# Five rotating PSUM banks in the retention, and feed-forward weights cast to bf16 ahead of time on the odd cores

## The chip, the cores and the metric

The kernel runs on the 8 cores of one Trainium2 chip as one program. The metric is the device time in microseconds of the slowest core. The runs of the kernel before took 2073.68, 2083.73 and 2284.54 us, median 2083.73.

## The reference

The input is `x`, four sequences of 2048 tokens by 2048 channels. What is computed:

```
xn = layernorm(x)
s  = retention(xn)          # 16 heads of 128: q, k, v = xn @ w_qkv; rotary tables on q and k;
                            # scores q k^T with a decay mask, causal; y = scores v;
                            # per-head norm (mean, variance); silu(xn @ w_g) * y; @ w_proj
r  = argmax(xn @ w_router)  # per token: one of three paths
g  = silu( path 0: xn + bias
           path 1: xn + (xn @ w_down^T) @ w_up^T
           path 2: transformer layer: layernorm, softmax attention (16 heads), residual,
                   layernorm, gelu(x @ w_ff1^T) @ w_ff2^T (8192 hidden), residual )
out = x + s * g
```

The weights come as float32 in DRAM. Products run in bf16. Path 2 is computed only for the tokens that take it (its queries and its feed-forward); its keys and values need every token of the sequence.

## The kernel before, in words

**Split.** Each sequence belongs to two cores. The even core (`FIRST`, names `a_`) has the first 1280 tokens, with 10 token tiles of keys and 10 of its own rows; the odd core (`SECOND`, names `b_`) has the last 768 tokens as its own and all 16 tiles of keys. The path-2 tokens are packed into 464 columns on an even core, 288 on an odd one. A branch on the input `half` picks the share; both are one program text.

**Stages.** (1) Phase 0: layernorm of the token tiles, transposes into `xn`, values of heads 0 to 3, and keys and queries of head 0. (2) Retention, `ret_step(h)` for 16 heads (L886 on). The main products of a step, 16 matmuls each into one PSUM bank (`group`, L252; the matmul is L262), are queries `Q` and keys `K` of head h+1 and the gate `G` of head h-1: 9 on an even core, 8 on an odd. After heads 3, 7 and 11 a burst `ret_vburst` computes the values of the next four heads (10 or 16 more products). (3) Projection `proj`, (4) attention of path 2, `ffn_step`, (5) `wo`, (6) `ff1` and `ff2`: 64 + 64 weight tiles, each of which feeds 16 matmuls of 464 or 288 columns.

**Order inside a step.** `gap(main)` runs one main product, then the deferred small pieces of the one before (`pend`, above all `swap`: the rotary partner product through L269, whose result VectorE multiplies into `swt` and adds), then `late`. Behind each gap come the small events of `ret_events`, at fixed slots: `T` transposes keys (L762), `U` the state (L776), `S(p)` a score pair (L796, L797), `A(p)` scores by values into bank Y (L816 to L822), `M` and `V` mean and variance of the head norm. Every engine executes its own instructions in this order.

**PSUM.** 8 banks: A, B and M rotate (`bank`, L244) among all main products and most small ones; Y takes the attention output; `S[0]` and `S[1]` are pairs of banks, used in turn by the scores (`s = p % 2`) and, `S[1]`, by the key transposes. A product waits until the engine that reads its bank has emptied it (`self.free[k]`). The cosine product `t_c` in `ret_qk` is issued to VectorE right after the main product's copy, ahead of the `swap` of the product before.

**Beside it.** In heads 0 to 3 VectorE also does the router: 80 pieces on an even core, 48 on an odd, two per event from gap 2 of head 0 on, the rest in the burst after head 3. In heads 4 to 11 `h_step` computes the path-1 and path-0 rows, in pairs (`h_first`, 2 small matmuls, L712, and 4 VectorE operations into `hz`): a step's first 6 (4) rows at gap 0, the others at gap nq+1, their silu at gaps nq and nq+2, the next loads at nq+2 and nq+4 (nq is 3 or 2).

**DMA.** Weight tiles are 128 by 2048, 1 MB in float32. GpSimd's queue (POOLq, queue q0) casts them on the way into SBUF, 0.5 MB there. Retention weights go through a ring `wr` of 5 (4) slots: a slot is reloaded when its product is done. The value weights are loaded one quarter per head, at the start of the step. From the last heads of path 2's attention on, `Ring` `wb` streams 16 + 128 tiles (`fo`, `f1`, `f2`) through 21 (28) slots. SyncE's queue (q1) moves rotary tables, router rows and intermediate results.

Of the kernel before, what the change touches and what calls it, by code (L numbers as in the profile page):

```python
# [36 lines left out]
class Share:  # L37
# [18 lines left out]
    wr=[6, 10, 14, 18, 22], xn=26, xt=[86, 66, 74], xk=[94, 98], og=66,  # L56
# [13 lines left out]
    wr=[6, 10, 14, 18], xn=22, xt=[86, 94, 102], xk=[110, 114], og=86,  # L70
# [66 lines left out]
class Ring:  # L137
# [17 lines left out]
    def load(self):  # L155
        while self.next < len(self.plan):
            k = self.next
            if k < self.n:
                if k not in self.opened:
                    return  # L160
                toks = self.opened[k]
            else:
                before = self.plan[k - self.n][0]
                if before not in self.freed:
                    return
                toks = (self.freed[before],)
            key, src = self.plan[k]
            t = self.kern.dma("pool", self.stream[k % self.n], self.tile[k % self.n][:, :], src,
                              *toks)
            self.got[key] = (self.tile[k % self.n], t)  # L170
            self.next += 1
# [6 lines left out]
class Kern:  # L178
# [92 lines left out]

    def gap(self, main):


        due, self.pend = self.pend, []
        main()
        for f in due:
            f()
        late, self.late = self.late, []
        for f in late:  # L280
            f()
# [7 lines left out]
    def build(self):  # L289
# [22 lines left out]
        self.xc_sp = dint("xc_sp", [CT, P, W])  # L312
        self.r_sp = dint("r_sp", [16, P], F32)
# [39 lines left out]
        self.S = [nc.alloc_psum_tensor(f"S{i}", [P, 2, W], F32) for i in range(2)]  # L353

# [28 lines left out]
    def run(self, s):  # L383
        nc = self.nc
        self.g, self.tag = s, s.name + "_"
        self.free = {k: None for k in "ABMY"}
# [46 lines left out]
    def phase0(self):  # L433
# [88 lines left out]
        self.t_p0 = [*xfree, *kfree]  # L522
        self.hq_load(0)
# [20 lines left out]
    def ret_buffers(self):  # L544
# [38 lines left out]
        self.main_last = None  # L583

# [13 lines left out]
    def ret_qk(self, kind, h, c, piece, col, w, dst):  # L598
# [13 lines left out]
        t_c = self.op("dve", "tt", dst, qb, tab[:, 0, 0:w], op=ALU.mult,  # L612
                      toks=(t_b, self.t_tab[h, piece], used))
        tmp = self.swt[n % 2][:, 0:w]

# [138 lines left out]
    def ret_kturn(self, h):  # L754

        n = self.g.parts[1][1]
        kk = self.kk[h % 2]
        out = self.S[1].ap().rearrange("p a n -> p (a n)").bitcast(BF16)[:, 0:n * P]
        self.wait("pe", self.Sfree[1], *[self.t_qk["k", h, c]
                                         for c, (col, w) in enumerate(self.g.kc) if col < n * P])  # L760
# [5 lines left out]
        self.t_kt = self.Sfree[1] = self.op("act", "act", self.kt[:, :], out, AF.Copy,  # L766
                                            toks=(tp, self.kt_used))
# [17 lines left out]
    def ret_score(self, h, p):  # L785
        g = self.g
        c, j, skip, w = g.pairs[p]
        s = p % 2
        S, n = self.S[s], self.nsc
# [3 lines left out]
        self.wait("pe", self.Sfree[s], self.t_qk["q", h, c], self.t_qk["k", h, j * P // W],  # L793
# [5 lines left out]
        self.Sfree[s] = self.op("dve", "tt", self.sc[n % 4][:, :, 0:w], S[:, :, 0:w],  # L799
                                self.mk[:, :, 0:w], op=ALU.mult, toks=(ts, self.sc_used[n % 4]))  # L800
        self.t_sc[h, p] = (self.Sfree[s], n % 4)
# [65 lines left out]
    def ret_events(self, h):  # L867
# [7 lines left out]
        if last == 2:  # L875
            ev = [[T], [S(0)], [S(1), U], [S(2), A(0)], [S(3), A(1)], [S(4), A(2)],
                  [A(3), M(0)], [A(4)], [V(0), M(1)], [], [V(1), M(2)], [], [V(2)]]
        else:
            ev = [[S(0)], [T], [S(1)], [U], [S(2)], [A(0)], [A(1)], [A(2)],
                  [M(0)], [], [V(0), M(1)], [], [V(1)]]  # L880
        return ev

    def ret_step(self, h):
# [25 lines left out]
        n = len(mains)  # L909
        steps = nq * 2 + len(g.kc)  # L910
        ev = self.ret_events(h)
        rest = self.ret_events(h - 1)[steps:] if h > 0 else []
        now = [(ev[k] + (rest[k] if k < len(rest) else [])) for k in range(steps)]
        by_gap = [[e for k, e in enumerate(now) if k * n // steps == a] for a in range(n)]
        for a, main in enumerate(mains):
# [8 lines left out]
            for e in by_gap[a]:  # L924
                if h < 4 and (h > 0 or a >= 2):
                    self.router_piece()
                for f in e:
                    f()
                if h < 4 and (h > 0 or a >= 2):
# [248 lines left out]
    def proj(self):  # L1178
# [44 lines left out]
        for k in range(n):  # L1223
# [4 lines left out]
            if rest and k > 0:  # L1228
                rest.pop(0)()
            if k >= 1:  # L1230
# [61 lines left out]
    def ffn_buffers(self):  # L1292
# [27 lines left out]
        if r > 0:  # L1320
            self.ffn_ring(r, self.t_x1c)
        plan = ([(f"fo{k}", self.wd["fo"][k]) for k in range(16)] +
                [(f"f1{k}", self.wd["f1"][k]) for k in range(FT)] +
                [(f"f2{k}", self.wd["f2"][k]) for k in range(FT)])
        self.big = Ring(self, f"wb{r}", "wb", [kb for part in m["big"] for kb in part], plan)
# [362 lines left out]
    def ff1(self):  # L1688
# [13 lines left out]
        self.wait("pe", *self.free.values(), *self.Sfree)  # L1702
# [147 lines left out]
```

How the kernel before makes its waits and increments, by code:

```python
    def wait(self, e, *toks):  # L197
        for tok in toks:
            if tok is None:
                continue
            s, v = tok
            if self.met[e].get(s.name, 0) < v:
                self.eng[e].wait_ge(s, v)
                self.met[e][s.name] = v
# [1 line left out]
    def done(self, e, inst):  # L206
        s = self.sem[e]
        inst.then_inc(s, 1)
        self.count[s.name] += 1
        return (s, self.count[s.name])
# [1 line left out]
    def dma(self, e, stream, out, in_, *toks, **kw):  # L212
        if stream not in self.dsem:
            self.dsem[stream] = self.new_sem("d_" + stream)
        s = self.dsem[stream]
        self.wait(e, *toks)
        self.eng[e].dma_start(out=out, in_=in_, **kw).then_inc(s, 16)
        self.count[s.name] += 16
        return (s, self.count[s.name])
# [1 line left out]
    def indirect(self, stream, out, out_at, in_, in_at, *toks, **kw):  # L221
        if stream not in self.dsem:
            self.dsem[stream] = self.new_sem("d_" + stream)
        s = self.dsem[stream]
        self.wait("pool", *toks)
        self.nc.gpsimd.indirect_dma_start(out, out_at, in_, in_at, **kw).then_inc(s, 16)
        self.count[s.name] += 16
        return (s, self.count[s.name])
```

## Time and profile before

| | us |
|---|---|
| runs | 2073.68, 2083.73, 2284.54 |
| profiled execution, time | 2068.31 |
| its spans, cores 0 to 7 | 1995.6, 2062.9, 1994.6, 2063.2, 1997.9, 2066.7, 1988.3, 2064.5 |
| granted TensorE clock, even / odd cores | 0.966 to 0.970 / 0.955 to 0.957 |
| core 5 (slowest): TensorE busy | 1749.7 |
| core 5: VectorE, ScalarE, GpSimd busy | 825.2, 678.1, 174.1 |

The span of a core is from its first to its last instruction. "Idle before" is the time an engine stood still just ahead of an instruction, and the releaser is what it waited for. A matmul's recorded length overlaps its neighbours, so the pitch from start to start is its cost in a full stream. The DMA share is the mean busy share of the core's 16 DMA engines.

### The profile page before, as it was taken

How to read it: one execution, taken by the hardware profiler on the slowest of the kernel's cores; microseconds unless marked ns; L12 is line 12 of the kernel's file. 1: busy time of each engine (PE TensorE's matmuls, PEld its weight loads, DVE VectorE, ACT ScalarE, POOL GpSimd, SP SyncE). 2: the span in 40 equal slices, each digit the busy share in tenths (PEclk: the TensorE clock that was granted, in tenths of full speed). 3: DMA queues.
4: the chain of work that ended last, by engine and by line, in shares of the span. 5: the costliest groups of instructions: out<-in, count | busy, mean ns of one | idle time of the engine just before them, and what ended most of it. 6: DMA issues, size and time to landing. Idle time of an engine off the chain costs nothing.

```text
span 2066.7 us, 28135 instructions; the slowest of 8 cores (1988.3 to 2066.7 us)
## 1 busy us (share of the span) xinstructions
PE 1749.7 (85%) x10020; PEld 954.1 (46%) x10020; DVE 825.2 (40%) x1502; ACT 678.1 (33%) x1099; POOL 174.1 (8%) x309
## 2 busy tenths in 40 slices
PE   4885689788897789987889999999999788876886
PEld 2442344444444344443344455555554456644554
DVE  4635671344414442242621356665657742000000
ACT  2431341233304431344752344444444523110000
POOL 0000000000000000000000000000001121211211
PEclk9996899999999999999999999999999989999998
DMA  8666751355645541432572435545435499999998
GB/s 205 216 95 159 178 143 31 66 106 104 143 142 106 110 92 34 91 83 51 116 169 51 87 67 94 101 87 108 87 67 108 78 173 171 170 165 170 200 213 164
DMA packets 105643, 247.95 MB, mean 120 GB/s; under 512 B 13970, under 2 KB 41874, under 8 KB 103314
## 3 DMA queue, kind: packets, MB, share of 16 engines
q0 software_dynamic: 42672, 149.18, 42.5%
q1 hardware_dynamic: 60754, 96.79, 16.7%
q8 instruction: 87, 1.43, 0.3%
q14 instruction: 66, 0.54, 0.1%
q10 hardware_dynamic: 2064, 0.01, 0.1%
HBM read 361.92 MB, written 27.67 MB: 189 GB/s over the span
## 4 chain that ended last, share of the span: by engine, by line
PE 69%; DVE 9%; ACT 6%; issue 6%; DMA 5%; another core or an unknown queue 4%; SPq 0%; DVEq 0%; POOL 0%; POOLq 0%; ACTq 0%
PE pA L262 20%; PE pM L262 17%; PE pB L262 16%; ACT L247 2%; PE pB L1751 2%; PE pM L1751 2%; DMA b_tab<-tab 1%; DVE b_t L247 1%; PE pA L1751 1%; ACT b_rs L247 1%; DVE b_lt L247 1%; PE pM L1197 1%; DVE bst L456 1%; DMA b_wrh<-wr 1%
## 5 line engine op out<-in xcount | busy, mean ns | idle before, releaser
L262 PE MATMUL pA<-b_vw,b_xn 128*128 128x512 bf16 x800 | 182.7, 382 | 8.6 <-DMA b_vw<-rv 8.6
L262 PE MATMUL pB<-b_xn,b_wr 128*128 128x512 bf16 (+1 forms) x752 | 156.6, 364 | 16.1 <-DVE b_t L247 9.0
L262 PE MATMUL pA<-b_xn,b_wr 128*128 128x512 bf16 (+1 forms) x672 | 147.5, 375 | 12.1 <-DVE b_t L247 8.3
L262 PE MATMUL pM<-b_vw,b_xn 128*128 128x512 bf16 x656 | 149.1, 380 | 0.0
L262 PE MATMUL pM<-b_xn,b_wr 128*128 128x512 bf16 (+1 forms) x656 | 134.3, 360 | 15.4 <-DVE b_t L247 7.3
L247 DVE TENSOR_TENSOR S<-S,b_cb 128x576 f32<-128x576 f32 x128 | 97.0, 760 | 122.5 <-PE S L1421 122.5
L262 PE MATMUL pB<-b_vw,b_xn 128*128 128x512 bf16 x592 | 133.8, 379 | 0.0
L262 PEld LDWEIGHTS pA<-b_vw,b_xn 128*128 128x128 bf16 x800 | 78.5, 98 | 98.7 <-issue 11.3
L262 PEld LDWEIGHTS pB<-b_xn,b_wr 128*128 128x128 bf16 x752 | 74.1, 101 | 86.3 <-issue 33.2
L247 ACT ACTIVATE b_er<-S 128x576 bf16<-128x576 f32 x128 | 83.2, 650 | 77.7 <-DVE S L247 77.3
L247 ACT ACT_TABLE_LOAD x65 | 83.4, 1283 | 63.4 <-PE pA L262 13.7
L262 PEld LDWEIGHTS pA<-b_xn,b_wr 128*128 128x128 bf16 x672 | 66.2, 100 | 82.1 <-issue 25.0
L262 PEld LDWEIGHTS pM<-b_xn,b_wr 128*128 128x128 bf16 x656 | 64.0, 100 | 75.2 <-issue 26.4
L262 PEld LDWEIGHTS pM<-b_vw,b_xn 128*128 128x128 bf16 x656 | 64.2, 98 | 74.6 <-issue 1.1
L262 PE MATMUL pA<-b_xn,b_wf 128*128 128x512 bf16 x416 | 94.0, 379 | 1.1
L217 POOL DMA_DIRECT2D b_wb<-f x128 | 68.2, 552 | 255.0 <-PE pM L262 40.6
L247 DVE TENSOR_TENSOR b_kk<-b_qkb,b_tab 128x512 bf16<-128x512 bf16 x64 | 27.2, 424 | 154.8 <-ACT b_qkb L247 152.2
L262 PEld LDWEIGHTS pB<-b_vw,b_xn 128*128 128x128 bf16 x592 | 57.5, 98 | 66.6 <-issue 0.3
L262 PE MATMUL pM<-b_xn,b_wf 128*128 128x512 bf16 x368 | 83.2, 379 | 0.0
L247 DVE TENSOR_TENSOR b_acc<-b_acc,b_er 128x576 f32<-128x576 f32 x96 | 72.8, 758 | 10.7 <-DVE b_er L247 0.9
L247 ACT ACTIVATE b_sq<-b_t 128x512 bf16<-128x512 f32 (+1 forms) x32 | 16.8, 525 | 140.3 <-DVE b_t L247 137.8
L262 PEld LDWEIGHTS pA<-b_xn,b_wf 128*128 128x128 bf16 x416 | 40.0, 98 | 47.7 <-issue 3.5
(319 smaller groups left out, 2723.5 us busy)
## 6 DMA issues: line engine op xcount, KB each, us to landing
b_wb<-f POOLq DMA_DIRECT2D x128, 512.0 KB, 68.9
b_tab<-tab SPq DMA_DIRECT2D x96, 256.0 KB, 4.0
b_xt<-xp SPq DMA_DIRECT2D x10, 1024.0 KB, 7.7
b_vw<-rv POOLq DMA_DIRECT2D x16, 512.0 KB, 10.4
b_wr<-rq POOLq DMA_DIRECT2D x16, 512.0 KB, 7.3
b_wr<-rk POOLq DMA_DIRECT2D x16, 512.0 KB, 5.9
b_wr<-rg POOLq DMA_DIRECT2D x16, 512.0 KB, 5.9
xn_sp<-b_xn SPq DMA_DIRECT2D x4, 2048.0 KB, 16.0
```

Source lines behind the costliest of these rows:

```text
L217: self.eng[e].dma_start(out=out, in_=in_, **kw).then_inc(s, 16)
L247: return self.done(e, f(*args, **kw))
L262: inst = self.nc.tensor.matmul(self.pb[k][:, 0:w], lhs(ct), rhs(ct), start=(ct == 0), stop=(ct == CT - 1))
L456: ins = nc.vector.bn_stats(b[:, 6 * q:6 * q + 6], xt[n % 3][:, q * W:(q + 1) * W])
L1197: self.nc.tensor.matmul(self.pb[b][:, :], self.og[:, hh, i * P:(i + 1) * P], w[:, hh, :], start=(hh == 0), stop=False)
L1751: ins = nc.tensor.matmul(self.pb[b][:, 0:sl], w[:, (ft % 16) * P:(ft % 16 + 1) * P], self.hg[ft][:, :], start=(ft == 0), stop=(ft == FT - 1))
```

## The change

- Once phase 0 is over, the two banks of `S[1]` join the rotation as X and Z, until the seventh unit of the projection (`pair_to_banks`, `banks_to_pair`). Scores and key transposes all use `S[0]`.
- The cosine product moves behind the `swap` of the product before (`late`).
- `h_first` comes one pair per gap instead of in bursts; the second silu and the load of the next columns' constants come at gap nq+3.
- Events of the head before come ahead of this head's; `M` and `V` events move one or two slots.
- Router pieces start with gap 6 of head 0. Head 0 has 6 gaps, so they start with head 1. In the value burst after head 3 all copies of values are ScalarE's.
- On odd cores (`cast=96`) the steps of heads 2 to 13 each issue, ahead of their main products, 8 DMAs on GpSimd's queue that cast a float32 tile in DRAM to a bf16 tile in DRAM (`fb_sp`). These 96 tiles are `f1` 16 to 63 and `f2` 0 to 47. The ring `wb` later loads them from there; `fo`, `f1` 0 to 15 and `f2` 48 to 63 stay float32.

```diff
-    wr=[6, 10, 14, 18, 22], xn=26, ...
+    wr=[6, 10, 14, 18, 22], cast=0, xn=26, ...
-    wr=[6, 10, 14, 18], xn=22, ...
+    wr=[6, 10, 14, 18], cast=96, xn=22, ...
...
+    def pair_to_banks(self):
+        self.free["X"] = self.free["Z"] = self.Sfree[1]
+        self.rot += ["X", "Z"]
+
+    def banks_to_pair(self):
+        self.wait("pe", self.free["X"], self.free["Z"])
+        self.rot = [k for k in self.rot if k in "ABM"]
+        self.Sfree[1] = None
...
+        self.fb_sp = dint("fb_sp", [96, P, C])
...
+        self.pb["X"], self.pb["Z"] = self.S[1][:, 0, :], self.S[1][:, 1, :]
...
+    def cast(self):
+        n = len(self.t_cast)
+        if 8 * n >= self.g.m["cast"]:
+            return
+        for k in range(8 * n, 8 * n + 8):
+            t = self.dma("pool", f"cast{n % 3}", self.fb_sp[k], self.ff_tile(k),
+                         self.t_cast[n - 3] if n >= 3 else None)
+        self.t_cast.append(t)
+
+    def ff_tile(self, k):
+        n = 16 + k
+        return self.wd["f1"][n] if n < FT else self.wd["f2"][n - FT]
+
+    def ff_plan(self):
+        plan = [(f"fo{k}", self.wd["fo"][k]) for k in range(16)]
+        for n in range(2 * FT):
+            key, src = ...
+            k = n - 16
+            plan.append((key, self.fb_sp[k], self.t_cast[k // 8])
+                        if 0 <= k < self.g.m["cast"] else (key, src))
+        return plan
...
@@ ret_qk
-        t_c = self.op("dve", "tt", dst, qb, tab[:, 0, 0:w], op=ALU.mult,
-                      toks=(t_b, self.t_tab[h, piece], used))
+        t_c = None
+        def cos():
+            nonlocal t_c
+            t_c = self.op("dve", "tt", dst, qb, tab[:, 0, 0:w], op=ALU.mult,
+                          toks=(t_b, self.t_tab[h, piece], used))
+        self.late.append(cos)
@@ h_step
-        if gap in (0, nq + 1):
-            for u in list(then if gap else first)[::2]:
-                self.h_first(u)
-        if gap in (nq, nq + 2):
+        for u in [u for k, u in enumerate(first[::2]) if k == gap]:
+            self.h_first(u)
+        for u in [u for k, u in enumerate(then[::2]) if k == gap - nq - 1]:
+            self.h_first(u)
+        if gap in (nq, nq + 3):
...
-        if gap == nq + 2 and q < 7:
+        if gap == nq + 3 and q < 7:
             self.hq_load(q + 1)
@@ ret_kturn: S[1], Sfree[1] become S[0], Sfree[0]
@@ ret_score
-        s = p % 2
-        S, n = self.S[s], self.nsc
+        S, n = self.S[0], self.nsc
@@ ret_events (first: even cores, second: odd cores)
-                  [A(3), M(0)], [A(4)], [V(0), M(1)], [], [V(1), M(2)], [], [V(2)]]
+                  [A(3), M(0)], [A(4)], [V(0)], [], [M(1)], [], [V(1)], [M(2)], [], [V(2)]]
-                  [M(0)], [], [V(0), M(1)], [], [V(1)]]
+                  [M(0)], [], [V(0)], [M(1)], [], [V(1)]]
@@ ret_step
+        if h >= 2:
+            self.cast()
...
-        now = [(ev[k] + (rest[k] if k < len(rest) else [])) for k in range(steps)]
+        now = [((rest[k] if k < len(rest) else []) + ev[k]) for k in range(steps)]
...
-                if h < 4 and (h > 0 or a >= 2):
+                if h < 4 and (h > 0 or a >= 6):
                     self.router_piece()
@@ ret_vburst
-            self.gap(lambda: self.ret_v(gr, i, "act" if i % 2 else "dve"))
+            self.gap(lambda: self.ret_v(gr, i, "act" if i % 2 or gr == 1 else "dve"))
@@ proj
+            if k == 6:
+                self.banks_to_pair()
```

## Rows read from the trace of the kernel before

**Rows 1.** Spans and granted clocks of cores; core 4 is even, core 5 odd.
```profile
core 4: 1997.9 us, clock 0.966
core 5: 2066.7 us, clock 0.956
```
**Rows 2.** Busy time by stretch, core 5: stretch, length, then each engine, clock, DMA share, GB/s.
```profile
1735.00:1790.00 55.00, 54.96 (x436) 43.38 (x437) 0.00 (x0) 12.24 (x32) 16.32 (x31) 0.97 1.04 172
1790.00:1880.00 90.00, 63.07 (x468) 44.38 (x466) 0.25 (x2) 12.24 (x30) 15.85 (x30) 0.98 1.04 168
1880.00:2051.00 171.00, 138.76 (x1063) 99.49 (x1060) 11.99 (x26) 7.51 (x15) 32.63 (x45) 0.99 1.06 200
```
**Rows 3.** Timeline of core 5's TensorE: start, length, instruction, idle before and its releaser.
```profile
1785.70 2.12 PE L262 MATMUL pA<-b_x2n,b_wb 128*128 128x288 bf16 x16
1787.66 2.12 PE L262 MATMUL pB<-b_x2n,b_wb 128*128 128x288 bf16 x16
...
2048.59 2.12 PE L1751 MATMUL pB<-b_hg,b_wb 128*128 128x288 bf16 x16 [0.33 <-DMA b_wb<-f]
```
**Rows 4.** Busy time by stretch, core 4, final stage.
```profile
1700.00:1800.00 100.00, 100.00 (x515) 50.09 (x514) 2.04 (x5) 15.84 (x27) 16.90 (x32) 1.00 1.04 170
```
**Rows 5.** DMA queues of core 5, whole span: packets, MB, share of 16 engines.
```profile
q0 software_dynamic: 42672, 149.18, 42.5%
q1 hardware_dynamic: 60754, 96.79, 16.7%
```
**Rows 6.** What TensorE of core 4 waited for, 170 to 960 us: total, times, longest.
```profile
PE pM L262 <- ACT a_sil L247: 13.2, 10, 1.6
PE pM L262 <- DVE a_swt L247: 11.9, 12, 2.7
```
**Rows 7.** Busy time of one head step, core 4: with shadow products, then without.
```profile
590.50:634.20 43.70, 36.63 (x206) 19.14 (x205) 25.81 (x52) 21.11 (x37) 2.64 (x5) 0.96 0.52 118
751.40:788.50 37.10, 33.45 (x197) 17.92 (x196) 16.31 (x30) 17.37 (x27) 1.59 (x3) 1.00 0.62 125
```
**Rows 8.** The same two kinds of step on core 5.
```profile
664.50:708.90 44.40, 34.60 (x189) 17.73 (x188) 19.26 (x40) 17.18 (x28) 2.64 (x5) 0.92 0.51 105
880.60:916.80 36.20, 32.14 (x182) 16.70 (x181) 14.06 (x28) 15.35 (x22) 1.58 (x3) 0.95 0.40 88
```
**Rows 9.** Timeline of core 4 about a score: VectorE's queue and TensorE's bank wait.
```profile
614.61 1.91 PE L262 MATMUL pM<-a_xn,a_wr 128*128 128x256 bf16 x16 [1.60 <-ACT a_sil L247]
615.24 0.48 DVE L247 SCALAR_TENSOR_TENSOR a_hz<-pA,msk,a_hk 128x256 f32<-128x256 f32 x1
...
616.46 0.27 PE L797 MATMUL S<-a_qq,a_kk 128*128 128x256 bf16 x1
...
620.16 0.69 DVE L247 TENSOR_TENSOR a_sc<-S,cblk 128x512 bf16<-128x512 f32 x1
```
**Rows 10.** What VectorE waited for, core 5, 141 to 400 us.
```profile
DVE b_qq L247 <- DMA b_tab<-tab: 29.6, 1, 29.6
...
DVE b_rj L247 <- DMA b_wrh<-wr: 10.7, 3, 6.1
```
**Rows 11.** One router piece on VectorE, core 5.
```profile
183.87 1.28 DVE L247 SCALAR_TENSOR_TENSOR b_rj<-b_rx,mv,b_wrh 128x1024 bf16<-128x1024 f32 x1
```
**Rows 12.** DMA queues of core 5, 664.5 to 708.9 us.
```profile
q0 software_dynamic: 719, 2.16, 30.2%
q1 hardware_dynamic: 2721, 2.46, 20.3%
```
**Rows 13.** GpSimd's issues of one head step, core 5.
```profile
699.48 0.53 POOL L217 DMA_DIRECT2D b_vw<-rv  x1 [0.26 <-issue]
709.15 0.53 POOL L217 DMA_DIRECT2D b_wr<-rg  x1 [9.13 <-PE pB L269]
719.29 0.53 POOL L217 DMA_DIRECT2D b_wr<-rk  x1 [9.61 <-PE pA L262]
```
**Rows 14.** Main products of a value burst in the chain of waits, core 5.
```profile
830.71 3.45 PE pM L262 x16
```

More of the change, by code:

```diff
@@ L55 @@
               [(0, 512), (512, 512), (1024, 256)], [(0, 4), (4, 8)], [0, 1, 2], dict(
-    wr=[6, 10, 14, 18, 22], xn=26, xt=[86, 66, 74], xk=[94, 98], og=66,
+    wr=[6, 10, 14, 18, 22], cast=0, xn=26, xt=[86, 66, 74], xk=[94, 98], og=66,
     rx=78, wrh=86, rj=98, xkh=100, iota=84, sel=86, hz=96, nhz=6, hk=102,
@@ L69 @@
                [(1280, 512), (1792, 256)], [(0, 10), (10, 14)], [1, 2], dict(
-    wr=[6, 10, 14, 18], xn=22, xt=[86, 94, 102], xk=[110, 114], og=86,
+    wr=[6, 10, 14, 18], cast=96, xn=22, xt=[86, 94, 102], xk=[110, 114], og=86,
     rx=92, wrh=100, rj=112, xkh=114, iota=98, sel=100, hz=106, nhz=4, hk=110,
@@ L166, in load @@
                 toks = (self.freed[before],)
-            key, src = self.plan[k]
+            key, src, *ready = self.plan[k]
             t = self.kern.dma("pool", self.stream[k % self.n], self.tile[k % self.n][:, :], src,
-                              *toks)
+                              *toks, *ready)
             self.got[key] = (self.tile[k % self.n], t)
@@ L385, in run @@
         self.g, self.tag = s, s.name + "_"
-        self.free = {k: None for k in "ABMY"}
+        self.free = {k: None for k in "ABMYXZ"}
         self.Sfree = [None, None]
@@ L522, in phase0 @@
         self.t_p0 = [*xfree, *kfree]
+        self.pair_to_banks()
         self.hq_load(0)
@@ L583, in ret_buffers @@
         self.main_last = None
+        self.t_cast = []
+    def cast(self):
[12 more added lines that the diff above has]
+        for n in range(2 * FT):
+            key, src = (f"f1{n}", self.wd["f1"][n]) if n < FT else (f"f2{n - FT}",
+                                                                   self.wd["f2"][n - FT])
+            k = n - 16
+            plan.append((key, self.fb_sp[k], self.t_cast[k // 8])
+                        if 0 <= k < self.g.m["cast"] else (key, src))
+        return plan
     def vw_load(self, which, g, tok, pieces=range(4)):
@@ L757, in ret_kturn @@
         kk = self.kk[h % 2]
-        out = self.S[1].ap().rearrange("p a n -> p (a n)").bitcast(BF16)[:, 0:n * P]
-        self.wait("pe", self.Sfree[1], *[self.t_qk["k", h, c]
+        out = self.S[0].ap().rearrange("p a n -> p (a n)").bitcast(BF16)[:, 0:n * P]
+        self.wait("pe", self.Sfree[0], *[self.t_qk["k", h, c]
                                          for c, (col, w) in enumerate(self.g.kc) if col < n * P])
@@ L765, in ret_kturn @@
         self.kk_used[h % 2] = tp
-        self.t_kt = self.Sfree[1] = self.op("act", "act", self.kt[:, :], out, AF.Copy,
+        self.t_kt = self.Sfree[0] = self.op("act", "act", self.kt[:, :], out, AF.Copy,
                                             toks=(tp, self.kt_used))
@@ L792, in ret_score @@
         q = self.qq[h % 2][:, col:col + w]
-        self.wait("pe", self.Sfree[s], self.t_qk["q", h, c], self.t_qk["k", h, j * P // W],
+        self.wait("pe", self.Sfree[0], self.t_qk["q", h, c], self.t_qk["k", h, j * P // W],
                   self.t_qk["k", h, (j + 1) * P // W])
@@ L798, in ret_score @@
             S[:, 1, 0:w], kk[:, (j + 1) * P:(j + 2) * P], q, start=True, stop=True))
-        self.Sfree[s] = self.op("dve", "tt", self.sc[n % 4][:, :, 0:w], S[:, :, 0:w],
+        self.Sfree[0] = self.op("dve", "tt", self.sc[n % 4][:, :, 0:w], S[:, :, 0:w],
                                 self.mk[:, :, 0:w], op=ALU.mult, toks=(ts, self.sc_used[n % 4]))
-        self.t_sc[h, p] = (self.Sfree[s], n % 4)
+        self.t_sc[h, p] = (self.Sfree[0], n % 4)
         self.qq_used[h % 2] = self.kk_used[h % 2] = ts
@@ L928, in ret_step @@
                     f()
-                if h < 4 and (h > 0 or a >= 2):
+                if h < 4 and (h > 0 or a >= 6):
                     self.router_piece()
@@ L1321, in ffn_buffers @@
             self.ffn_ring(r, self.t_x1c)
[L1322 to L1325, printed above, removed]
+        self.big = Ring(self, f"wb{r}", "wb", [kb for part in m["big"] for kb in part],
+                        self.ff_plan())
     def big_open(self, part, *toks):
@@ L1701, in ff1 @@
                 [self.S[s][:, a, 0:sl] for s in (1, 0) for a in range(2)])
-        self.wait("pe", *self.free.values(), *self.Sfree)
+        self.wait("pe", *[self.free[k] for k in "ABMY"], *self.Sfree)
         for ct in range(CT):
```

## The prediction

> **What bounds the kernel now.** First the spans: the odd cores end last, 2066.7 us against 1997.9 on the even core of the same pair [rows 1]. So 68.8 us of any gain on odd cores count, and beyond that both kinds must gain.
>
> Next the busy time by stretch of the odd core's feed-forward. TensorE is busy 54.96 of 55 us up to 1790, then 63.07 of 90 and 138.76 of 171, while the DMA share stays at 1.03 to 1.06 [rows 2]. The timeline says how long a weight tile takes TensorE when nothing is missing: starts at 1785.70 and 1787.66, a pitch of 1.96 us. At the end each tile waits for its load [rows 3]. From 1790 on the odd core waits for weights. The even core, with 464 columns per tile, is busy 100.00 of 100 us there [rows 4]: nothing in this stage can speed it up.
>
> Then the retention. A head step of the even core takes 43.70 us with 36.63 busy; without the small products of path 0 and 1 it takes 37.10 with 33.45 busy [rows 7]. On the odd core it is 44.40 with 34.60 at a clock of 0.92, and 36.20 with 32.14 [rows 8]. The waits of the even core name readers of banks A, B and M: ScalarE's silu and VectorE's rotary product [rows 6]. TensorE is ready and lacks a bank.
>
> **The tail of the odd core.** Queue q0 moved 149.18 MB, as written, in 42.5% of 2066.7 us, so a tile of 0.524 MB costs 3.09 us [rows 5]. That is what a cast load costs. An uncast bf16 tile is not in this queue; half as many bytes are read for it, so 1.54 us is one bound. The other is queue q1's rate, which includes its small packets: 345 us for 96.79 MB, 1.87 us per tile [rows 5]. Both are below 1.96, so the choice changes nothing: TensorE sets the pace. From 1735 us 120 tiles remain, which end at 2051 now [rows 2]. At 1.96 us they take 235, and 48 transposes about 5: 1735 + 240 = 1975, **76 us less**. The last 16 float32 tiles need 49 us of DMA against 31 of products, but 28 slots let them start 28 x 1.96 = 55 us early. Their cover is gone only if the ring starts late.
>
> **Five banks and the new order.** For the even core the floor of a step is its busy time at full clock, 36.63 x 0.96 = 35.2 us [rows 7]. Against it stands the single score pair. Today a score ends at 616.73 and its mask product at 620.85, 4.1 us later, since VectorE has `hz` operations of 0.48 us ahead of it [rows 9]. With two pairs nobody waits for that. With one, the next score or key transpose does. In the new order the VectorE work of gap 0 or 1 adds up to about 5.4 us (rotary 1.5, one pair of rows 2.0, mean 0.7, mask 1.2), and the next product is partly the 256-column one, so about 2 us per step stay lost. I take 37.0 for the even core: 8 steps x 6.7 = 54 us. In heads 12 to 14 `h_first` is absent; I take 34.7, which gives 3 x 2.4 = 7. Head 0 sheds 12 router pieces of 1.28 us [rows 11], which return in the value burst, where ScalarE takes over the copies; I take 8. The 29.6 us wait for a rotary table [rows 10] stays, since that load stands behind the same router loads. Sum **70 us**: 1998 to 1928. The bounds are 85 (no pinch) and 20 (a pinch in most gaps).
>
> On the odd core the same working gives 34.60 x 0.92 = 31.8, with the pinch and some hiccups 34.5: 8 x 9.9 = 79; heads 12 to 14 to 32, 3 x 4 = 12; head 0 8. Sum 99, before the casts.
>
> **The casts.** GpSimd issues 8 x 0.53 us per head; it stood idle 9 us before its next issue, so this hides [rows 13]. The wait on an earlier cast is met a head before. The DMA time does not hide as well. The trace has no DRAM-to-DRAM cast. The nearest row is the cast load, with the same read and the same bytes written: 3.09 us. If the write came on top at q1's rate it would be 3.09 + 1.87 = 4.96. I take 3.1, since in the load too reading and writing run together; nothing excludes less, to the 1.54 of half the work.
>
> In a step the two queues use 30.2 + 20.3% of 44.4 us, 22.4 us [rows 12]. With 24.8 of casts it is 47.2, more than the 34.5 that TensorE would need. Over four heads with a burst of 14 products of 3.45 us, 48 us [rows 14], the demand is 189 us against 186. So the burst pays back, but the three steps before it cannot all be short: 34.5, then about 42 and 45. That returns 18 us per group, 36 in heads 4 to 11. In head 2 of the odd core the second set of router weights now loads amid a cast; VectorE's wait of 10.7 us [rows 10] becomes about 20: 9 us. Sum 45. The odd core keeps 99 - 45 = **54 us** of the retention.
>
> All casts and the next weights share GpSimd's queue. The gate tile of the next step is issued 9.7 us after the step's first load, the key tile 10.1 later [rows 13]. Behind a cast batch they land about 30 us into the step and are needed near 40. The Trainium skill ("DMA: Bandwidth & Descriptors", section SWDGE vs HWDGE vs iDMA) says that only one SWDGE queue is allocated, so this order cannot be escaped; the trace agrees, with all of GpSimd's loads in q0.
>
> **Sum.** Odd: 2066.7 - 76 - 54 = 1937. Even: 1928. The profiled execution took 2068.31, 1.6 more than its span; two of the runs shown lie 5 and 15 above it, the third far off. So 1937 + 1.6 + 10 = 1949, say **1950**.
>
> **Rivals.**
> *Casts are dear (0.14).* The DMA share during the cast heads goes to 1 and TensorE waits for ring tiles. At 4.4 us a cast, a step needs 22.4 + 35.2 = 57.6 us of DMA and a group of four 230, against 226 now (4 x 44.4 + 48): heads 4 to 11 gain nothing. Head 0 and heads 12 to 14 keep 20, head 2 loses 10 and heads 12 and 13, with less DMA of their own, 8. Odd: 2066.7 - 76 - 20 + 18 = 1989, time 2000; at the upper bound 4.96 a group costs 248, 44 more in two groups, time about 2045. For it: the three steps are already short of DMA at 3.1. Against: a tile of the load costs 3.09 us for 1 MB read and half of that written, and q1 1.87 for as much written and half as much read [rows 5]; that looks like a price set by the longer side. The same page (section Specifications) limits a core to about 358 GB/s of HBM. By it, the 1.57 MB that a cast reads and writes would take 4.4 us, an estimate; the feed-forward's rows, about 170 GB/s written and twice that read, do not contradict it.
> *The score pair takes the place of the banks (0.10).* If VectorE's lag stays at 4.1 us, a score behind a short product waits about 2.4 us, and the order of events forces five such places a step: the even core gains nothing and ends at 1998, time 2010. For it: the pair is used by five scores and a transpose. Against: the bursts of `h_first`, which cause the lag, are gone.
> *Slower: the casts cost far more than a load (0.06).* Place: queue q0 in heads 2 to 13, 670 us now, of which 12 x 22.4 = 269 are demanded by today's DMAs. The tail's 76 us are eaten at (670 + 76 - 269) / 96 = 5.0 us a cast; 2% slower is 5.4. At 6.2, twice the load, it is 864 us: time about 2190. Against it: the row bound is 4.96.
> *The tail is not relieved (0.04).* If the ring still arrives late, for instance because bf16 tiles cost near 3 us, only the retention gains: 2067 - 54, time about 2025.
>
> **Chances.** My forecast has 0.66. What a measurement here can tell from no change is about 2%, 42 us: faster means below 2042. Of the rivals the dear casts fall mostly there (0.09 of 0.14), the pair and the tail almost wholly: faster 0.88, same 0.06, slower 0.06. Range: low, no loss to the casts and no pinch, where the even core at 1913 decides: 1905 allows for its last microseconds. High, the pair rival and the middle of the dear casts: 2025.
>
> **What would show it.** Right: on odd cores the feed-forward from 1735's counterpart on at a pitch of 1.96 us per tile, DMA share well under 1 there; head steps of 37 us on the even core, 6.7 less than now; on the odd core short steps after a burst and longer ones before the next, with waits on `wr` tiles; both kinds of core within 30 us of each other. Wrong: TensorE waiting for `wb` loads still, L796 or L762 waiting for VectorE's `sc` more than 3 us a step, cast DMAs that take over 4 us each in the queue, or rotary tables that land so late beside them that the odd core's steps are over 44 us.

## The result, and the profile after

The changed kernel takes 2172.08 us (median of 4 runs, 2143.39 to 2332.38) where the kernel before takes 2088.01 in the same session (4 runs): the ratio is 1.0316, with an interval of 1.0228 to 1.0404. It is slower; 1950 was forecast. The far ends of these ranges are executions at a lower clock on one die, which the ratios and the mean spans given below leave out and the medians do not.

Spans and granted clocks, to be set against [rows 1]:

```profile
core 6: 2042.5 us, clock 0.949
core 7: 2141.8 us, clock 0.919
```

Core 7 is odd, core 6 even; the other cores of each kind lie within 9 and 6 us of them. The odd core is 75.1 us longer than core 5 before, the even one 44.6 longer than core 4. Both lost, the odd one more.

Where? I cut each core's time at two marks of the timeline: the transposes of the keys of head 0 and of head 15. These are the marks of core 7, then those of core 5 before:

```profile
142.39 0.94 PE L807 MATMUL S<-cblk,b_kk 128*128 128x128 bf16 x14 [2.28 <-DVE b_sc L247]
1104.24 0.94 PE L807 MATMUL S<-cblk,b_kk 128*128 128x128 bf16 x14 [2.56 <-DVE b_sc L247]
```
```profile
141.00 0.94 PE L762 MATMUL S<-cblk,b_kk 128*128 128x128 bf16 x14
950.10 0.94 PE L762 MATMUL S<-cblk,b_kk 128*128 128x128 bf16 x14 [0.83 <-DVE b_kk L247]
```

Before head 0 nothing changed (+1.4 us). Heads 0 to 15 grew from 809 to 962, **+153**. What follows, to the end of the span, shrank from 1116.6 to 1037.6, **-79**. The even core does the heads in 800 us against 767, +33, and what follows in 1146 against 1135, +11.

**The tail.** Busy time by stretch, core 7, answering [rows 2]:

```profile
1900.00:2000.00 100.00, 100.00 (x819) 79.88 (x817) 0.00 (x0) 20.96 (x51) 26.92 (x51) 1.00 0.97 318
2000.00:2100.00 100.00, 100.00 (x836) 80.25 (x835) 10.95 (x25) 7.01 (x14) 28.84 (x43) 1.00 0.87 213
```

From the first tile of `ff1` to the last of `ff2` core 5 takes 237.4 us (1886.3 to 2123.7), against 315.4 before (1735.0 to 2050.4): 78 us less. TensorE is busy 100.00 of 100 us, where core 5 had 138.76 of 171. Its timeline has the pitch of 1.96 us of [rows 3], now without a wait:

```profile
1951.06 2.12 PE L262 MATMUL pM<-b_x2n,b_wb 128*128 128x288 bf16 x16
1953.02 2.12 PE L262 MATMUL pA<-b_x2n,b_wb 128*128 128x288 bf16 x16
```

**The heads of the odd core.** Two steps of core 7, answering [rows 8]; the transposes at their edges are 89.7 and 37.8 us apart:

```profile
421.00:511.00 90.00, 36.20 (x190) 18.80 (x191) 19.64 (x41) 17.05 (x28) 6.55 (x13) 0.71 0.95 150
511.00:548.00 37.00, 33.59 (x205) 18.41 (x202) 20.30 (x45) 16.96 (x28) 6.65 (x13) 0.93 0.51 102
```

The second is the forecast step, 37 us with 33.59 busy. The first has almost the same work and takes 90. The granted clock averages 0.71 over it: TensorE stands still for tens of us and comes back at the lower of its two levels, half of full speed. From 520 us on it is at full speed again:

```profile
507.00:512.00 5.00, 1.26 (x13) 1.29 (x14) 4.62 (x10) 0.90 (x2) 0.00 (x0) 0.50 0.49 159
...
520.00:530.00 10.00, 8.06 (x51) 4.22 (x50) 4.52 (x9) 6.43 (x12) 1.06 (x2) 1.00 0.51 101
```

Step by step against core 7 of experiment 1, the same order without casts: head 2 takes 53 us more, head 4 53, head 6 59, head 10 30, and each of the others 12 or less. Three steps of twelve make two thirds of the loss. Why head 5, with the same eight casts, loses only 3 us is not explained.

What TensorE and VectorE of core 7 wait for, from 170 and from 90 us to 1105:

```profile
PE S L807 <- DVE b_sc L247: 176.7, 15, 48.3
PE S L840 <- DVE b_sc L247: 39.3, 7, 19.3
PE S L756 <- DMA b_hu<-up: 22.8, 2, 13.8
```
```profile
DVE b_hz L247 <- DMA b_hk<-xk_sp: 169.4, 8, 61.0
DVE b_xkh L247 <- DMA xk_sp<-b_xkh: 37.0, 3, 21.6
```

The heaviest lines of the two engines are for the most part one wait. TensorE waits at the transposes (L807) for the mask product that frees the only score pair. That product stands in VectorE's queue behind an `hz` operation, which waits for a tile `hk` of 64 KB, up to 61 us. The timeline of GpSimd, SyncE, VectorE and TensorE in the long step shows the chain:

```profile
456.55 3.89 POOL L217 DMA_DIRECT2D fb_sp<-f  x8 [0.19 <-issue]
...
467.47 38.47 SPq L217 DMA_DIRECT2D b_hk<-xk_sp  x6
...
506.74 0.48 DVE L247 SCALAR_TENSOR_TENSOR b_hz<-S,msk,b_hk 128x256 f32<-128x256 f32 x1 [46.04 <-DMA b_hk<-xk_sp]
...
509.38 1.22 DVE L247 TENSOR_TENSOR b_sc<-S,cblk 128x1024 bf16<-128x1024 f32 x1
...
510.74 1.55 PE L807 MATMUL S<-cblk,b_kk 128*128 128x128 bf16 x13 [37.65 <-DVE b_sc L247]
```

Eight casts are issued at 456. SyncE needs 38 us for six loads of `hk`, since each waits for the store that empties its buffer (`h_sp<-b_hk`), and that store is late as well. What SyncE waited for from 467 to 507 us:

```profile
SPq L203 <- DMA h_sp<-b_hk: 35.5, 6, 18.5
```

VectorE stands 46 us and TensorE 38. The DMA issues of 455 to 512 us (count, KB each, median us to landing) say what was in the way:

```profile
fb_sp<-f POOLq DMA_DIRECT2D x8, 512.0 KB, 30.5
b_tab<-tab SPq DMA_DIRECT2D x4, 256.0 KB, 3.6
...
b_wr<-rg POOLq DMA_DIRECT2D x1, 512.0 KB, 32.1
b_hk<-xk_sp SPq DMA_DIRECT2D x6, 64.0 KB, 31.7
```

**The heads of the even core.** The step that answers [rows 7], and TensorE's waits of 170 to 960 us, which answer [rows 6]:

```profile
568.00:612.00 44.00, 36.37 (x202) 20.03 (x204) 25.38 (x50) 20.32 (x37) 2.64 (x5) 0.92 0.72 76
```
```profile
PE S L840 <- DVE a_sc L247: 102.6, 30, 9.3
...
PE pB L269 <- ACT a_yb L247: 6.4, 3, 5.5
```

The long list of waits for a reader of A, B or M is gone, as planned. One wait for the single score pair has taken its place.

### The profile page after: what moved, and what is told of

Read it like the earlier page. It is cut to its first block, busy times and chain, and to the rows that moved or that the text cites. A ratio compares the mean times of both kernels' runs of the same rounds, so it can differ in the third digit from the quotient of the medians.

```text
span 2141.8 us, 28220 instructions; the slowest of 8 cores (2037.0 to 2141.8 us)
## 1 busy us (share of the span) xinstructions
PE 1725.8 (81%) x10020; PEld 958.7 (45%) x10020; DVE 817.6 (38%) x1494; ACT 681.6 (32%) x1107; POOL 221.2 (10%) x405
## 4 chain that ended last, share of the span: by engine, by line
PE 60%; DMA 18%; DVE 8%; issue 5%; SPq 4%; ACT 4%; another core or an unknown queue 1%; POOL 0%; DVEq 0%; POOLq 0%; ACTq 0%
PE pM L262 13%; PE pB L262 13%; PE pA L262 11%; PE S L262 6%; DMA b_hk<-xk_sp 5%; DMA h_sp<-b_hk 4%; SPq L217 4%; DMA b_rx<-xp 3%; PE pA L1797 2%; DMA b_wr<-rg 2%; PE pM L1797 2%; PE pB L1797 2%; DMA b_tab<-tab 1%; DVE b_lt L247 1%; DVE bst L467 1%
## 5 line engine op out<-in xcount | busy, mean ns | idle before, releaser
L262 PE MATMUL S<-b_xn,b_wr 128*128 128x512 bf16 (+1 forms) x880 | 190.7, 374 | 13.7 <-ACT b_rs L247 7.7
L807 PE MATMUL S<-cblk,b_kk 128*128 128x128 bf16 x224 | 18.6, 247 | 179.0 <-DVE b_sc L247 179.0
L262 PEld LDWEIGHTS S<-b_xn,b_wr 128*128 128x128 bf16 x880 | 89.4, 103 | 99.2 <-issue 33.7
L262 PE MATMUL pA<-b_vw,b_xn 128*128 128x512 bf16 x480 | 111.0, 385 | 10.0 <-DMA b_vw<-rv 10.0
L262 PE MATMUL pB<-b_xn,b_wr 128*128 128x512 bf16 (+1 forms) x480 | 100.1, 364 | 7.7 <-DMA b_wr<-rg 7.7
L807 PEld LDWEIGHTS S<-cblk,b_kk 128*128 128x128 bf16 x224 | 15.8, 111 | 184.2 <-issue 184.2
L262 PE MATMUL pM<-b_xn,b_wr 128*128 128x512 bf16 (+1 forms) x320 | 73.8, 388 | 11.7 <-DMA b_wr<-rg 9.7
L262 PE MATMUL pB<-b_xn,b_wf 128*128 128x512 bf16 x368 | 83.2, 379 | 0.0
L262 PE MATMUL pA<-b_xn,b_wr 128*128 128x512 bf16 (+1 forms) x400 | 79.2, 353 | 4.4 <-ACT b_rs L247 4.4
L262 PEld LDWEIGHTS pA<-b_vw,b_xn 128*128 128x128 bf16 x480 | 47.2, 99 | 65.7 <-issue 13.6
L262 PEld LDWEIGHTS pB<-b_xn,b_wr 128*128 128x128 bf16 x480 | 47.7, 101 | 51.5 <-issue 15.0
L262 PE MATMUL S<-b_vw,b_xn 128*128 128x512 bf16 x304 | 67.4, 379 | 0.0
```

Source lines behind the costliest of these rows:

```text
L262: inst = self.nc.tensor.matmul(self.pb[k][:, 0:w], lhs(ct), rhs(ct), start=(ct == 0), stop=(ct == CT - 1))
```

## The experiments

Twelve kernels ran, in three sessions; the kernel before took 2067.85, 2067.54 and 2069.15 us in them, with mean spans of 2062 us on odd cores and 1992 to 1993 on even ones. "Heads" below is the time from the transpose of head 0 to that of head 15, as above, in the traced execution; kernel 5 is the kernel of experiment 5.

**1. The retention change alone.** One word: `cast=96` becomes `cast=0`.

> The changed kernel without the casts (no tile is cast ahead; every feed-forward weight is loaded as float32). Theory A, one score pair: the new retention order itself is slower, since scores and key transposes wait for the one pair. On even cores nothing differs from the changed kernel, so they stay near 2040 us; the odd cores end near 2067 + 30 = 2095 us. Ratio to before about 1.01. Theory B, the casts alone are to blame and they slow the even cores too, through the shared HBM: then even cores fall below 1998 us here and odd cores below 2067, ratio 0.96 to 0.99.

2019.81 us, ratio 0.9773 (0.9753 to 0.9792). Odd spans 1989 to 2002, even 2006 to 2029. The means are 1998 and 2015: the retention change gives 64 us on odd cores and takes 22 on even ones. The odd cores do as theory B said; the even ones as neither. Odd heads take 715 to 726, 86 less than before. TensorE's waits of even core 6, 170 to 850 us, with nobody casting:

```profile
PE S L840 <- DVE a_sc L247: 84.4, 31, 5.7
```

Below, a head step of that core and then one of core 4 before:

```profile
598.00:644.00 46.00, 37.18 (x210) 20.56 (x213) 26.59 (x53) 20.77 (x38) 2.64 (x5) 0.93 0.52 112
```
```profile
590.00:634.00 44.00, 36.73 (x205) 19.23 (x205) 26.00 (x54) 21.11 (x37) 2.64 (x5) 0.96 0.52 119
```

**2. The casts alone.** The kernel before with

```
+        if h >= 2:
+            self.cast()
```

> The kernel before with the casts alone (old order, three rotating banks, two score pairs; 96 tiles cast on odd cores). Theory A, the casts block SyncE's small transfers: head steps 2 to 13 of the odd cores are longer by some 60 to 120 us in sum, with VectorE waiting for b_hk, and the feed-forward gives back 75; odd cores end at 2050 to 2110, even cores unchanged at 1998. Rival, only the meeting of casts and the single score pair costs time: with two pairs the odd cores lose at most 20 us in the heads and end near 2067 - 55 = 2012.

2126.91 us, ratio 1.0208 (1.013 to 1.0286). The traced execution, of 2133.82 us, has odd heads of 887 to 951, 930 on average against 808. In the two quickest executions, of 2101.37 and 2120.00 us, the odd cores average 2085 us against 2062. The part behind the heads gives back 75 (1040 against 1115), so the heads come to about 905 there, an estimate. The casts thus cost some 100 to 120 us with the old retention, and 233 with the new one (956 - 723, the middle of the four odd cores each). Theory A holds, and its rival does not: casts cost time with two pairs as well. But the new retention about doubles their price. VectorE's waits for `hk` come to 58 us on core 7 and 100 on core 1, against 169 in the change. Whether the single pair, the shorter steps or the new places of `h_first` and of the `hk` loads do this, no run tells.

**3 and 4. The same bytes in small packets.** A cast tile is a whole stretch of memory on both sides, and the trace of core 7 has 16 packets of 32768 bytes for each; core 7 moved 12288 packets in q0 for 80.69 MB in its heads. With rows 2176 columns apart the core makes 24624 packets for 86.45 MB:

```
-        self.fb_sp = dint("fb_sp", [96, P, C])
+        self.fb_sp = dint("fb_sp", [96, P, C + P])[:, :, 0:C]
```

Experiment 3 is the whole change with it:

> The changed kernel with one edit: the rows of the bf16 copy in DRAM are 2176 elements apart instead of 2048, so that a cast tile can't be moved in pieces longer than one row. Same bytes, same places in the program. Theory A, the 32768-byte packets of the casts (3.06 us each on a DMA engine) let the small packets of SyncE's queue pass only one by one: with 4096-byte packets b_hk lands within 10 us, VectorE's 169 us of waits for it fall below 50, odd cores end 60 to 120 us earlier, near 2040. Rival, it is the amount of DMA work: the work is the same, so the odd cores stay within 15 us of 2142.

2076.45 us, ratio 1.0042 (1.0028 to 1.0056). Odd spans 2068 to 2072, 70 less than the change; odd heads 886 to 892. The DMA queues of core 7, 170 to 1105 us, of the change and of this kernel:

```profile
q0 software_dynamic: 12288, 80.69, 53.5%
```
```profile
q0 software_dynamic: 24624, 86.45, 56.7%
```

The work is no less, yet 70 us are back. VectorE's wait for `hk` falls from 169.4 to 119.5, the longest from 61 to 52. So the size has a part, but neither case came: the theory wanted waits below 50 us and odd cores near 2040, the rival no change. Experiment 4 is the casts in small packets on the kernel before:

> The kernel before with the casts alone, their rows apart as in the run above. Theory A, packet size: the odd cores lose at most 25 us in the heads against before and gain 75 in the feed-forward, and end near 2015; even cores at 1998. Rival, amount of DMA work: as in the run with the casts alone and packed rows, 2050 to 2110.

2098.06 us, ratio 1.0147 (1.0098 to 1.0197). The traced execution, the fastest of the four with 2068.60 us, has odd heads of 865 to 887. That can't be set against the traced one of experiment 2, which was among its longer ones. In the two quickest executions of each, the odd cores average 2061 and 2085 us, 23 apart, while single cores vary by 50 to 60, and the intervals of the two ratios overlap. So with the old retention a gain by small packets is likely and not shown. The theory (odd cores near 2015) did not come.

**5. The casts in the attention,** large packets, six ahead of each of the 16 heads of the next stage:

```
 def ffn_step(self, h):
+        self.cast()          # 6 instead of 8 a call
 def ret_step(self, h):
-        if h >= 2:
-            self.cast()
```

> The changed kernel with its 96 casts (in their large packets, as in the change) issued in the attention of the feed-forward layer, 6 at the start of each of its 16 heads, instead of 8 in each of heads 2 to 13 of the retention. Theory (the casts cost time because they stand among the small transfers on which the retention's heads wait, not by their bytes): the odd cores keep the spans of the retention change alone (2001) less the 75 us of the tail, 1926 to 1945; the even cores, which cast nothing, stay at 2006 to 2029 and now end last, time 2010 to 2030. Rival (a cast costs its share of DMA wherever it is): some 1.5 to 2.2 us a tile, odd cores at 2070 or more.

2049.95 us, ratio 0.9921 (0.9903 to 0.9939). Odd heads are at 714 to 721, as without casts, so the retention pays nothing. But odd spans are 1997 to 2014, not 1926 to 1945: the theory missed by 70 us, and so did the rival, on the other side. Busy time by stretch on core 5:

```profile
1100.00:1200.00 100.00, 81.42 (x417) 40.73 (x416) 47.06 (x81) 33.54 (x60) 7.96 (x16) 0.91 0.95 163
...
1600.00:1700.00 100.00, 29.18 (x141) 14.55 (x138) 29.81 (x53) 15.28 (x27) 11.12 (x21) 0.64 1.00 176
```

With 6 casts of 3.2 us in each head of some 35 us, the DMA share of 0.33 to 0.54 that kernel 1 has in the attention becomes 0.88 to 0.98. The small transfers of this stage (`out_tok`, `b_yx`, `b_ys`) land after 22 to 25 us instead of 5. TensorE waits 55.4 us in all for exponentials' tiles `b_er`, and in the last stretch 46.8 us at once for `b_xr`. So the room of a stage can be used up: the place alone does not make casts free. The even cores, with the code of experiment 1, average 2039 us against 2015 there.

**6. Two score pairs, new order.** `pair_to_banks` and `banks_to_pair` are left out, the score goes to `self.S[p % 2]` and the transpose to `self.S[1]`; no casts.

> Nothing cast; the new order of the retention, but with banks A, B and M and both score pairs as before. Theory (the single score pair took the place of the banks on the even cores, 84 us of waits for the mask product in heads 1 to 15): the waits on a score pair go, and bank waits come back in part; even head steps fall from 44.5 to 40 to 43 us and even spans to 1970 to 2000; odd steps rise from 37 to about 41, odd spans from 2001 to about 2035. Rival (the order, not the pair, costs the even cores): even spans stay at 2010 to 2029.

2036.33 us, ratio 0.9853 (0.9836 to 0.9871). Odd as expected: spans 2030 to 2033, heads 758 to 760. Even: 2000 to 2010, heads 769 to 778, between the expectations. The pair waits went, others came. TensorE of even core 0, 170 to 960 us:

```profile
PE pY L860 <- ACT a_yb L247: 24.4, 22, 3.5
PE pA L262 <- ACT a_sil L247: 13.8, 10, 2.0
```

**7. The old retention on even cores,** the new one with the late casts of experiment 5 on odd ones (each changed line asks `self.new`, true for odd cores).

> Even cores with the retention as before the change in every part, odd cores with five banks, the new order and the casts issued in the attention. Theory: even spans 1998 as before, odd 1926 to 1945, time 2000, ratio 0.965 to 0.97 to the kernel before. Rival (the casts cost wherever they are): odd cores above 2050 and no gain.

2039.85 us, ratio 0.987 (0.9835 to 0.9905). Odd 2005 to 2020, as in 5. Even cores, whose code is that of before, take 2019 to 2035 in the traced execution. On average over all four they take 2029 us against 1993, 36 more. Neither case foresaw this.

**8. Casts in small packets, one ahead of each product** of a head instead of eight at its start:

```
-        for k in range(8 * n, 8 * n + 8):
+        k = 8 * n + a              # a: the gap
```

> The changed kernel with casts into rows that lie apart (4096-byte packets) and one cast ahead of each of a head's eight products instead of eight at the head's start. Theory (a batch of 25 us of transfers stands ahead of the ring's weight tiles and the head's small transfers, so the batch costs and not the sum): odd spans fall from 2068 to 2020 to 2045. Rival (the sum of the DMA work of a head costs, 47 us against a step of 37): no change beside the batch, 2060 to 2075. Second rival: GpSimd issues each cast later and the last products of a head still wait behind one, no more than 3 us a head either way.

2041.24 us, ratio 0.9866 (0.9839 to 0.9892). Odd spans 2009 to 2023, below the theory's 2020 to 2045; heads 831 to 843 against 886 to 892: the batch was worth 50 us. Steps still reach 64 us. One of core 5 has a DMA share of 1.04, so the sum of the work counts too:

```profile
396.00:460.00 64.00, 31.26 (x193) 17.43 (x194) 19.84 (x41) 17.15 (x28) 6.88 (x13) 0.79 1.04 166
```

**9. Even cores old, odd cores new, no casts.** As 7 with `cast=0`, and the even cores take over two of the new points: no router pieces in the first six gaps of head 0, and copies of the value burst on ScalarE.

> Nothing cast. Odd cores with the whole retention change, even cores with the retention as before in all but two points: the router pieces of head 0 move into the value burst, whose copies ScalarE makes. Theory (the retention change gives on odd cores and takes on even ones, where the score pair and a lower granted clock pay for the banks): odd 2001, even 1985 to 1998, time 2003 to 2008, ratio about 0.970. Rival (even cores gain only by chance of the chip's clock): even 2005 or more.

2002.1 us, ratio **0.9684** (0.9659 to 0.9708): the fastest of all, as the theory had it. Odd 1985 to 1991, even 1976 to 1997, on average 1995 and 1990 over four executions.

**10. Sixty casts where there is room.** Kernel 9 with 4096-byte packets, one cast beside each of 12 products in value bursts 2 and 3, and three in each of 12 attention heads. Each waits for a product or an exponential of its own place, and for the cast three before it:

```
+            if gr > 1 and i < 12:
+                self.cast(self.vw_last)
...
+            if h < 12 and a in (0, 3, 6):
+                self.cast(self.Sfree[0])
```

> The kernel of the previous expectation with 60 casts in 4096-byte packets on the odd cores: one beside each of 12 products in value bursts 2 and 3, and three in each of 12 heads of the attention, each held back by a wait for work of its own place. Theory (the casts cost where the DMA of a stage has no room, nothing where it has): the bursts use 0.11 to 0.32 of the DMA in their second halves and the attention 0.45, so the heads of the retention keep their 37 us, the tail gives 50 to 75, odd 1935 to 1965; the even cores end last at 1990 to 2010 and the time is 1995 to 2015. Rival (a cast costs 1.4 us or more in any place): odd 2001 - 60 + 84 = 2025 or more.

2026.78 us, ratio 0.9791 (0.976 to 0.9821). Spans:

```profile
core 2: 2014.8 us, clock 0.967
core 3: 1911.5 us, clock 0.971
```

The four odd cores end at 1912 to 1919, some 73 us before those of kernel 9, and below the expectation. Their heads take 710 to 721, and core 5 does not wait in the tail:

```profile
1700.00:1800.00 100.00, 100.00 (x825) 80.01 (x824) 4.40 (x11) 15.84 (x36) 27.32 (x51) 1.00 1.00 201
```

That is 4 us more than in kernel 9 (719 against 714, the middle of four cores). From the transpose of head 15 to the first tile of `ff1` core 5 takes 781 us against 784: in the attention the casts cost nothing. But the even cores end at 1999 to 2015; their means are 2012 us against 1990 in kernel 9, 22 more, and they set the time. So on odd cores the theory holds, with more gain than it named, and as a kernel it loses to 9. Kernel 10 differs from 5 in the number of casts, their packets, their batches, their places and their waits at once; which of these made them cheap was not tried one by one.

**11. Large packets, spread.** Kernel 8 with the packed rows.

> The changed kernel with one cast ahead of each of a head's eight products instead of eight at the start, in its own large packets: with the same in 4096-byte packets (odd 2009 to 2023), the batch in 4096-byte packets (2068) and the change itself (2133 to 2142) this makes a table of packet size against batch. Theory (a large packet holds each of the 16 engines for 3 us, and a small transfer of SyncE waits behind one in each of them, however few are queued): 40 to 70 us above the spread one in small packets, odd 2050 to 2090. Rival (the size counts only in a batch): 2010 to 2035.

2074.03 us, ratio 0.9953 (0.9911 to 0.9995). Odd spans 2026 to 2051, heads 845 to 874. The table of odd heads, the middle of the four cores of each kernel, is then:

| casts in the retention | large packets | 4096-byte packets |
|---|---|---|
| none | 723 | |
| 8 at a head's start | 956 | 888 |
| 1 ahead of each product | 865 | 836 |
| 24 in bursts, 36 in the attention | | 719 |

The size costs 68 us in a batch and 29 when spread: both my cases missed a little, the truth is between them. The batch costs 91 in large packets and 52 in small ones. The last 113 remain with small packets and no batch. Each cell is one traced execution, and the mean odd span of such a kernel varies by 5 to 15 us from one execution to the next.

**12. Five banks alone.** The kernel before with the banks and the single pair, old order, no casts.

> The kernel before with the five banks and the single score pair alone: nothing cast, the order of products, router pieces, h_first, rotary and copies as before. Theory (a single pair waits for VectorE's lag, 4.1 us before, which the old order with its bursts of h_first makes longer): waits on a score pair above 100 us on the even core, even spans 2010 to 2040, odd 2030 to 2060. Rival (five banks pay by themselves): even below 1990, odd below 2020.

2039.75 us, ratio 0.9862 (0.984 to 0.9884). Even spans 2020 to 2023, heads 794 to 797; odd 2034 to 2037, heads 762 to 764. TensorE of even core 0, 170 to 960 us:

```profile
PE S L839 <- DVE a_sc L247: 91.2, 34, 6.8
```

That is just below the 100 us expected, and the spans are in the expected ranges; the rival is out. The table of heads, in us, the middle of the four cores of each kernel:

| | odd | even |
|---|---|---|
| before | 808 | 764 |
| five banks alone | 763 | 795 |
| new order alone | 759 | 771 |
| both | 723 | 774 |

On an odd core each half gives 45 to 49 us and both give 85. On an even core five banks alone cost 31 us, the new order alone 7 and both 10: neither half pays there.

## Why the prediction was wrong, by its steps

**The tail: right.** 76 us were forecast and 78 came, at the pitch of 1.96 us. Only one sign missed: the DMA share was to be well under 1, and it was 0.97 and 0.87. The price of a cast tile's load can now be read. DMA issues of 1950 to 2050 us, core 7, its queue and its ring tiles:

```profile
q0 software_dynamic: 7712, 27.42, 88.6%
b_wb<-fb_sp POOLq DMA_DIRECT2D x47, 512.0 KB, 4.9
```

88.6 us for 27.42 MB, 52 tiles of 0.524 MB, make 1.69 us a tile, between the two bounds given. At least four float32 tiles are among them, so it is rather an upper bound.

**Odd cores, retention: nearly right.** Forecast 99 before the casts, measured 86 in the heads (experiment 1), in a step of 35 to 39 us against my 34.5. Of these 86 only 64 reached the span. The feed-forward there takes 333 us on core 5 against 315. It runs its loads together with those of the even cores to the end, at 164 to 175 GB/s, where core 5 alone had 200 in its last stretch [rows 2]. That this is the reason is argued, not shown.

**Even cores, retention: the step that failed second.** 70 us were forecast (the terms 54, 7 and 8 make 69), 54 of them from 37-us steps. In experiment 1 the heads of the even cores take 10 us more, in steps of 44 to 46 us. I had allowed a pinch of 2 us a step; the waits for the one pair come to 84 us. My rival (the score pair takes the place of the banks), at 0.10, named this wait and that the even core would gain nothing. It did not foresee that the same change would pay on odd cores.

But the single pair does not explain the loss alone. With both pairs back (experiment 6) the even heads take 771 us, still 7 more than before: other waits stand there, such as 24.4 us for the reader of bank Y. I had added up waits that go and one that comes, as if the order of events were free. Which wait would have to go for an even core to gain is open. The rows show one more difference: with waits of up to 6 us in one piece the granted clock of a step is 0.93, and with waits of mostly 1 to 3 us spread over the step it was 0.96. That the first causes the second is argued, not shown.

**The casts: the step that failed first, and decided.** The price of a cast was right: between 467 and 507 us q0 has

```profile
q0 software_dynamic: 646, 5.55, 86.9%
```

which is 34.8 us for 10.6 tiles' bytes, 3.28 us each, the eight casts and 2.6 ring tiles. By themselves the 1536 cast packets of core 7, 16 a cast, took 3.24 us each on one of 16 engines, so a cast costs 3.24 us against 3.1 forecast. The loss was to be 45 us; it was 233 in the heads (956 - 723). What failed is "47.2 us of DMA against 34.5 of products, so two steps of three grow to about 42 and 45". That treats DMA as one pool, in which only the sum counts. The head after a burst, forecast at 34.5 us, took 90, because work that is on the path, `hk` and its store, 64 KB each, stood behind work that is not. SyncE passes through store and load for six tiles in turn; a load lands after 31.7 us instead of 3.9 (the medians here and in experiment 1). The steps of heads 4 and 6 took 90 and 96 us so, while that of head 5 ran in 38. Head 2 was to lose 9 us and lost 53. There `hk` is not yet used: VectorE waited 37.0 us for the router's `xk_sp` stores and 21.6 for its rows `b_rx`, while the router weights that I had costed took 5.9. I costed ring tiles and rotary tables behind the casts; of `hk`, which was in the same rows, I said nothing.

Of the 233 us the table gives 68 to the packet size in a batch and 52 to the batch itself; 113 remain. They are still more than twice my 45, and their split is open. The sum of the DMA work is a part of them, as the share of 1.04 in a step of 64 us shows. But casts spread over the gaps are issued by GpSimd in the clusters that its waits for ring tiles make, and no run with evenly paced casts in these heads was made. Another cut through the same 233 us is by the retention: some 100 to 120 us are there with the old one (experiment 2).

In the same 40 us the eight casts read 1.05 MB and write 0.52 each, and the 2.6 ring tiles read 1.05 each: 15.3 MB, some 380 GB/s of DRAM traffic by this queue alone, an estimate. The Trainium skill ("DMA: Bandwidth & Descriptors", section Specifications) puts HBM at about 358 GB/s a core, by which a cast would take 4.4 us, an estimate. The row contradicts it as a limit for one core of a pair whose other core loads less (core 6 moved 105 to 106 GB/s in 400 to 500 us of its span).

**The slower rival.** It named casts of over 5.0 us in q0 as the point of decision. They cost 3.24 and the kernel was slower all the same, since the loss did not come from the price of a cast. Its sum would give the 153 us that the heads of core 7 lost only at 5.8 us a cast, (670 + 153 - 269) / 96. It also speaks of q0 but counts 22.4 us a step, which are both queues' [rows 12]. That "slower" came is no merit of its working.

**Why both kinds of core slow down.** Even cores cast nothing, and their heads went from 774 (experiment 1) to 802 in the change, their mean spans from 2015 to 2040. The same code on even cores, with and without casts on the odd ones, differs by 24 us in experiments 5 and 1, 36 in 7 and before, 22 in 10 and 9, but only by 5 and 6 in 2 and 4 and before. A forecast core by core has to give the partner's transfers a price.

**Wrong in the chances.** I gave 0.66 to a case that needed two uncertain sums to hold at once, and 0.06 to all that slows. Each of the failed steps had a sign in the rows: `hz` ahead of the mask product [rows 9], and a step in which DMA demand is above the step's length.

## What to carry to other kernels

Before bulk transfers are put into a stage, list the small transfers there whose landing some engine waits for, and ask what each costs if it lands after the whole batch. The sum of DMA work is a lower bound only: a step of 47 us by the sum took 96. Put the bulk where the DMA share is low and nothing small is awaited. With small packets and a wait of its place for each, 60 casts cost their core some 4 us so, and 96 at the heads' starts 233; which part of that recipe is needed was not tried. When a buffer pair is traded for single buffers, count the users of what is left, and the longest queue ahead of its reader; it can help one shape of core and hurt another, so let each have its own.

## What the runs showed of the hardware

- A contiguous DRAM-to-DRAM cast moves in large packets, 16 of 32768 bytes for a 512 KB tile, and takes 3.24 us of the 16 DMA engines. With padded rows, twice as many packets for about the same bytes, the whole kernel took 3% less (ratio 1.0042 against 1.0316); the rest of the program had not been touched.
- A queue of its own does not shield a transfer: loads of 64 KB from SyncE's queue landed after 31.7 us while eight 512 KB casts of GpSimd's queue were under way, and after 3.9 without casts.
- Cores slow each other without waiting for each other: even cores with unchanged code took 5 to 36 us longer on average when the odd ones cast as well. What they share, and whether it is only the other core of the pair, was not measured.
